# A two-layer graph network: masks laid out by pairs of target tiles, and raw adjacency quarters placed in mask places not yet filled

## The reference

```python
h = jnp.maximum(_layernorm(x, axis=-1), 0.0)
# layer 0
mask = (adj > 0).astype(x.dtype)
agg = mask @ h / jnp.maximum(jnp.sum(mask, axis=1, keepdims=True), 1.0)
combined = jnp.concatenate([h @ W_self + b_self, agg @ W_nb + b_nb], axis=-1)
x = x + jax.nn.relu(combined @ W_comb + b_comb)
h = jnp.maximum(_layernorm(x, axis=-1), 0.0)
# layer 1, per head: Wh = h @ W, sl = Wh . a_l, sr = Wh . a_r
e = jax.nn.leaky_relu(sl[:, :, None] + sr.T[None, :, :], negative_slope=0.2)
e = jnp.where((adj + I > 0)[:, None, :], e, -jnp.inf)
x = x + jax.nn.elu(softmax(e) @ Wh)
```

## Time and profile before

| | |
|---|---|
| median of 3 runs | 873.18 us (868.62 to 874.45) |
| the profiled execution | 872.05 us, span 870.5 us |
| PE busy | 799.2 us, 92% |
| DVE busy | 697.1 us, 80% |
| ACT busy | 564.1 us, 65% |
| transfers | 115.68 MB, mean 133 GB/s |
| first sum of the aggregation, last projection in it | 90.74 us, 369.30 us |

### The profile page before, as it was taken

How to read it: one execution, slowest core, us unless ns; L and a number is a source line. 1 busy time by engine, 2 the same in 40 slices (tenths; PEclk the granted TensorE clock), 3 DMA queues, 4 the chain that set the end, 5 groups by cost and what they waited for, 6 DMA issues and landing times.

```text
span 870.5 us, 26604 instructions
## 1 busy us (share of the span) xinstructions
PE 799.2 (92%) x10789; PEld 726.9 (84%) x10789; DVE 697.1 (80%) x1339; ACT 564.1 (65%) x839; POOL 138.1 (16%) x253
## 2 busy tenths in 40 slices
PE   5896898999999989969999999999999999999995
PEld 4342687778887878759999999999999999999995
DVE  3896766677776676587897999888999889998884
ACT  3574022222222222388999998999989999999991
POOL 0113234444444444400000000000000000000000
PEclk9999799999999999969999999999999999999998
DMA  8645999999999999440041012221101410112001
GB/s 212 181 145 142 281 277 289 285 307 318 316 304 296 300 298 295 101 107 26 1 96 48 2 47 49 49 49 47 48 6 43 96 48 8 41 49 48 9 16 37
DMA packets 91107, 115.68 MB, mean 133 GB/s; under 512 B 62608, under 2 KB 64464, under 8 KB 91056
## 3 DMA queue, kind: packets, MB, share of 16 engines
q1 hardware_dynamic: 70336, 61.57, 26.9%
q10 hardware_dynamic: 10784, 32.65, 13.5%
q0 software_dynamic: 9936, 20.86, 8.4%
HBM read 98.17 MB, written 16.85 MB: 132 GB/s over the span
## 4 chain that ended last, share of the span: by engine, by line
PE 39%; DVE 20%; DMA 17%; ACT 12%; issue 9%; POOL 1%; POOLq 0%; DVEq 0%; ACTq 0%
DMA rows<-own_scratch 14%; ACT stage L752 8%; PE ps_x L623 8%; PE ps_t L623 7%; PE ps_a L623 7%; PE ps_w L623 4%; PE ps_h L623 4%; DVE stage L1046 4%; DVE bits L940 2%; DMA stage<-in_adj 2%; DVE stage L1036 2%; PE ps_a L540 2%; DVE stage L1056 2%; PE ps_t L571 2%; PE ps_t L573 2%
## 5 line engine op out<-in xcount | busy, mean ns | idle before, releaser
L571 PE MATMUL ps_t<-g,mask 128*128 128x257 f16 x1024 | 230.3, 275 | 9.9 <-DVE mask L947 9.9
L573 PE MATMUL ps_t<-g,mask 128*128 128x256 f16 x1024 | 230.2, 273 | 0.0
L752 ACT ACTIVATE stage<-rows,sr 128x1024 int8<-128x1024 f32 x192 | 204.3, 1171 | 5.7 <-PE ps_w L623 5.7
L752 ACT ACTIVATE stage<-bits,sr 128x1024 int8<-128x1024 f32 x192 | 204.3, 1170 | 2.4 <-PE ps_w L623 2.4
L1046 DVE SCALAR_TENSOR_TENSOR stage<-stage,mask 128x1024 int32<-128x1024 int32 x128 | 156.9, 1225 | 22.1 <-ACT stage L752 21.4
L623 PE MATMUL ps_x<-g,stage 128*128 128x130 f16 x2048 | 158.7, 219 | 10.0 <-DVE stage L1056 4.8
L623 PE MATMUL ps_t<-g,stage 128*128 128x130 f16 x2048 | 158.4, 219 | 0.0
L623 PE MATMUL ps_a<-g,stage 128*128 128x130 f16 x2048 | 158.4, 219 | 0.0
L623 PEld LDWEIGHTS ps_x<-g,stage 128*128 128x128 fp8e4 x2048 | 127.4, 97 | 12.1 <-issue 12.0
L623 PEld LDWEIGHTS ps_a<-g,stage 128*128 128x128 fp8e4 x2048 | 127.3, 97 | 0.3
L623 PEld LDWEIGHTS ps_t<-g,stage 128*128 128x128 fp8e4 x2048 | 127.3, 97 | 0.2
(11 more groups left out here) (130 smaller groups left out, 838.9 us busy)
## 6 DMA issues: line engine op xcount, KB each, us to landing
stage<-in_adj SPq DMA_DIRECT2D x134, 256.0 KB, 7.4
stage<-in_adj ACTq DMA_DIRECT2D x122, 256.0 KB, 9.1
own_scratch<-mask POOLq DMA_DIRECT2D x16, 256.0 KB, 2.6
rows<-in_x POOLq DMA_DIRECT2D x128, 32.0 KB, 7.3
rows<-own_scratch POOLq DMA_DIRECT2D x32, 128.0 KB, 9.3
x_scratch<-late POOLq DMA_DIRECT2D x32, 128.0 KB, 7.3
bits<-s_scratch SPq DMA_DIRECT2D x8, 512.0 KB, 4.2
rows<-s_scratch SPq DMA_DIRECT2D x8, 512.0 KB, 4.7
```

The source lines that it names most:

```text
L571: nc.tensor.matmul(ps_t32[e][:, 0:D + 1], at, g[:, 2 * kk + b, D:2 * D + 1], start=kk + b == 0, stop=kk == NK - 1 and b == 1, skip_group_c ...
L573: last = nc.tensor.matmul(ps_t32[e][:, 0:D], at, g[:, 2 * kk + b, 0:D], start=False, stop=kk == NK - 1 and b == 1, skip_group_check=True)
L752: nc.scalar.activation(sign_bytes(sgn, k, b), srow[gr % 2], ACT.Sign, bias=sr[:, 2 * k + b, H + gr // NS:H + gr // NS + 1]).then_inc(act_s ...
```

## The change

The mask is now indexed by pair of target tiles first, then source pair, then the column within the pair: `mask[P, 16, 16, 2P]`. Target pair r has one contiguous row of 8 KB, which is exactly the size of a raw quarter. The prologue's tensors lie in rows 8 to 15 alone. Rows 1 to 7 are free from the start, and raw quarters wait there and, later, in other rows that aren't filled yet. There are 19 places for quarters (16 mask rows and the three of before); `SLOT[n]` names the place of quarter n and `LAST_IN[n]` the quarter that was in it before. `slot_free` holds the waits. SP issues a whole quarter (four parts) with the x rows of each of pairs 4 to 15, quarters 1 to 12, then quarter 13 whole; from 14 on the parts are shared with ScalarE again. ScalarE issues its halves of 14 to 17 at the end of its prologue and the others at the steps that `issued_at` gives.

The x rows of pairs 2 to 15 become one transfer instead of four. On POOL the loops are written out, `own` is fetched ahead of the four parts of x, and a tile's projection is stored ahead of the next tile's x1. The rings in `stage` and `stage2` keep the new order of the mask, with the same number of elements in every operation. `rows` holds own and x of a tile side by side.

Work and bytes are otherwise the same. In the diff blank lines and most context are left out, and the hunk on VectorE's `signs` too, whose only change is the same new view.

```diff
@@ -63,8 +63,8 @@
-ZR = 8
-PR = 4
+ZR = 4
+PR = 2
@@ -96,10 +96,11 @@
-            return mask[:, k, N // 2 + 2 * at:N // 2 + 2 * (at + n)].bitcast(F32)
-        mask = sb("mask", [P, NK, N], U16)
-        mask32 = mask[:, :, :].bitcast(I32)
+            first = NK // 2 * N + k * (N // 2) + 2 * at
+            return mask[:, :, :, :].rearrange("p r k n -> p (r k n)")[:, first:first + 2 * n].bitcast(F32)
+        mask = sb("mask", [P, NK, NK, 2 * P], U16)
+        mask32 = mask[:, :, :, :].bitcast(I32)
@@ -133,10 +134,11 @@
-        halves = [stage[:, 0, :], stage[:, 1, :], stage2[:, :]]
-        rows = sb("rows", [P, 4, D], F32)
-        own = rows[:, 0:2, :]
-        xt = rows[:, 2:4, :]
+        slots = ([mask32[:, r, :, :].rearrange("p k n -> p (k n)") for r in range(NK)]
+                 + [stage[:, 0, :], stage[:, 1, :], stage2[:, :]])
+        rows = sb("rows", [P, 2, 2 * D], F32)
+        own = rows[:, :, 0:D]
+        xt = rows[:, :, D:2 * D]
@@ -169,8 +171,8 @@
-        sgn = stage[:, :, :].rearrange("p f m -> p (f m)").bitcast(I8).rearrange("p (k n) -> p k n", k=ZR)
-        pos = stage2[:, :].rearrange("p (k n) -> p k n", k=PR)
+        sgn = stage[:, :, :].rearrange("p f m -> p (f m)").bitcast(I8).rearrange("p (q r k n) -> p q r k n", q=ZR, r=NJ // 2, k=2)
+        pos = stage2[:, :].rearrange("p (q r k n) -> p q r k n", q=PR, r=NJ // 2, k=2)
@@ -220,7 +222,7 @@
-        stage_in = [sem(f"stage_in{i}") for i in range(3)]
+        raw_in = [sem(f"raw_in{i}") for i in range(NK + 3)]
@@ -296,16 +298,41 @@
-            for a in range(UN):
-                eng.dma_start(xin[k % XR][a * UP:(a + 1) * UP, :], x_v[a, k]).then_inc(x_in[k % XR], 16)
+            if k < 2:
+                for a in range(UN):
+                    eng.dma_start(xin[k % XR][a * UP:(a + 1) * UP, :], x_v[a, k]).then_inc(x_in[k % XR], 16)
+            else:
+                eng.dma_start(xin[k % XR], x_v[:, k]).then_inc(x_in[k % XR], 16)
+        def x_landed(eng, k):
+            eng.wait_ge(x_in[k % XR], k // XR * 16 + (16 * UN if k % XR < 2 else 16))
+        def slot_free(eng, n):
+            if n == EARLY:
+                eng.wait_ge(wmm_ready, 2)
+            elif n == EARLY + 1:
+                eng.wait_ge(ab_ready, 4)
+                eng.wait_ge(consts, 5)
+            elif n == EARLY + 2:
+                eng.wait_ge(h_ready, NK)
+            elif n == EARLY + 3:
+                eng.wait_ge(hT_ready, NK)
+            elif n in (EARLY + 7, EARLY + 8, EARLY + 9):
+                eng.wait_ge(mm_free, 2 * NK + 4)
+            elif n == EARLY + 10:
+                eng.wait_ge(mm_free, 2 * NK + 4)
+                for b in range(2):
+                    eng.wait_ge(own_out[b], 16 * NP2)
+            elif n > EARLY:
+                eng.wait_ge(bits_ready, LAST_IN[n] + 1)
         def adj_rows(eng, n, parts):
-            if n >= 3:
-                eng.wait_ge(bits_ready, n - 2)
+            slot_free(eng, n)
             for a in parts:
-                eng.dma_start(halves[n % 3][a * UP:(a + 1) * UP, :].rearrange("p (e c) -> p e c", e=2),
-                              adj_v[n // UN, n % UN, a]).then_inc(stage_in[n % 3], 16)
+                eng.dma_start(slots[SLOT[n]][a * UP:(a + 1) * UP, :].rearrange("p (e c) -> p e c", e=2),
+                              adj_v[n // UN, n % UN, a]).then_inc(raw_in[SLOT[n]], 16)
@@ -338,10 +365,9 @@
-                if k in (XR, XR + 2):
-                    adj_rows(sp, (k - XR) // 2 + 1, range(UN))
-            for n in range(3, 2 * NT):
-                adj_rows(sp, n, range(UN // 2))
+                adj_rows(sp, k - XR + 1, range(UN))
+            for n in range(NK - XR + 1, 2 * NT):
+                adj_rows(sp, n, range(UN if n < BOTH else UN // 2))
@@ -436,57 +462,42 @@
-            def store_own(k, b):
+            def store_own(k):
                 pool.wait_ge(own_ready, k * 2 + 2)
-                pool.dma_start(own_d[bass.ds(k, 1)].rearrange("o p d -> p (o d)"), ownA[:, b, :]).then_inc(own_out[b], 16)
-            with pool.Fori(0, NP2 - 1) as i:
-                for b in range(2):
-                    store_own(i * 2 + b, b)
-            def row(k, e):
+                pool.dma_start(own_d[k], ownA[:, k % 2, :]).then_inc(own_out[k % 2], 16)
+            def row(t):
+                e = t % 2
+                pool.dma_start(own[:, e, :], own_d[t // 2, :, e * D:(e + 1) * D]).then_inc(row_in[e], 16)
                 for a in range(UN):
-                    pool.dma_start(xt[a * UP:(a + 1) * UP, e, :],
-                                   x_v[a, bass.ds(k, 1), :, e * D:(e + 1) * D].rearrange("o i d -> (o i) d")
+                    pool.dma_start(xt[a * UP:(a + 1) * UP, e, :], x_v[a, t // 2, :, e * D:(e + 1) * D]
                                    ).then_inc(row_in[e], 16)
-                pool.dma_start(own[:, e, :], own_d[bass.ds(k, 1), :, e * D:(e + 1) * D]
-                               .rearrange("o p d -> p (o d)")).then_inc(row_in[e], 16)
-            def store_x1(k, e):
-                pool.wait_ge(x1m_ready, k * 2 + (e + 1))
-                pool.dma_start(x1_d[bass.ds(k * 2 + e, 1)].rearrange("o p d -> p (o d)"), x1[:, e, :]
-                               ).then_inc(x1_out[e], 16)
-            def store_wh(t, e):
+            def store_x1(t):
+                pool.wait_ge(x1m_ready, t + 1)
+                pool.dma_start(x1_d[t], x1[:, t % 2, :]).then_inc(x1_out[t % 2], 16)
+            def store_wh(t):
                 pool.wait_ge(wh_ready, t + 1)
-                pool.dma_start(wh_d[bass.ds(t, 1)].rearrange("o p d -> p (o d)"), wh[:, e, :]
-                               ).then_inc(wh_out[e], 16)
+                pool.dma_start(wh_d[t], wh[:, t % 2, :]).then_inc(wh_out[t % 2], 16)
+            for k in range(NK - 2):
+                store_own(k)
             for b in range(2):
                 pool.wait_ge(own_out[b], 16 * (NP2 - 1))
-            row(0, 0)
-            row(0, 1)
-            for b in range(2):
-                store_own(NK - 2 + b, b)
+            row(0)
+            row(1)
+            store_own(NK - 2)
+            store_own(NK - 1)
             for b in range(2):
                 pool.wait_ge(own_out[b], 16 * NP2)
-            store_x1(0, 0)
-            row(1, 0)
-            with pool.Fori(1, NK - 1) as k:
-                store_x1(k - 1, 1)
-                row(k, 1)
-                store_wh(k * 2 - 2, 0)
-                store_x1(k, 0)
-                row(k + 1, 0)
-                store_wh(k * 2 - 1, 1)
-            store_x1(NK - 2, 1)
-            row(NK - 1, 1)
-            store_wh(NT - 4, 0)
-            store_x1(NK - 1, 0)
-            store_wh(NT - 3, 1)
-            store_x1(NK - 1, 1)
-            store_wh(NT - 2, 0)
+            for t in range(NT):
+                if t:
+                    store_wh(t - 1)
+                store_x1(t)
+                if t + 2 < NT:
+                    row(t + 2)
@@ -567,7 +578,7 @@
-                        at = bytes_of(mask32[:, kk, t // 2 * P:(t // 2 + 1) * P], e, b)
+                        at = bytes_of(mask32[:, t // 2, kk, :], e, b)
@@ -622,7 +633,7 @@
-                            bytes_of(ring[:, k % size, j // 2 * P:(j // 2 + 1) * P], j % 2, b),
+                            bytes_of(ring[:, q % size, j // 2, k % 2, :], j % 2, b),
@@ -704,7 +715,7 @@
-            for n in range(3, 9):
+            for n in range(BOTH, EARLY + 8):
@@ -732,11 +743,11 @@
-                if 2 * t + 9 < 2 * NT:
-                    adj_rows(act, 2 * t + 9, range(UN // 2, UN))
+                for n in issued_at(2 * t):
+                    adj_rows(act, n, range(UN // 2, UN))
-                if 2 * t + 10 < 2 * NT:
-                    adj_rows(act, 2 * t + 10, range(UN // 2, UN))
+                for n in issued_at(2 * t + 1):
+                    adj_rows(act, n, range(UN // 2, UN))
@@ -746,10 +757,10 @@
-                wait_pair(act, gr, q - ZR // 2)
+                wait_pair(act, gr, q - ZR)
-                    nc.scalar.activation(sign_bytes(sgn, k, b), srow[gr % 2], ACT.Sign,
+                    nc.scalar.activation(sign_bytes(sgn, k, b), srow[gr % 2].rearrange("p (r n) -> p r n", n=2 * P), ACT.Sign,
@@ -843,7 +854,7 @@
-                dve.wait_ge(x_in[k % XR], (k // XR + 1) * 16 * UN)
+                x_landed(dve, k)
@@ -934,17 +945,17 @@
-                dve.wait_ge(stage_in[n % 3], (n // 3 + 1) * 16 * UN)
+                dve.wait_ge(raw_in[SLOT[n]], SLOT[:n + 1].count(SLOT[n]) * 16 * UN)
-                                        halves[n % 3].rearrange("p (e m s) -> p e m s", e=2, s=2),
+                                        slots[SLOT[n]].rearrange("p (e m s) -> p e m s", e=2, s=2),
-                nc.vector.transpose(mask32[:, :, n * UP:(n + 1) * UP],
+                nc.vector.transpose(mask32[:, n // UN, :, n % UN * UP:(n % UN + 1) * UP],
@@ -992,7 +1003,7 @@
-                blk = mask32[:, k, k * P:(k + 1) * P]
+                blk = mask32[:, k, k, :]
@@ -1041,20 +1052,21 @@
```

(43 more changed lines are left out.)

## The result

The changed kernel takes 914.99 us in the median of four runs (911.89 to 917.63), beside 872.93 for the kernel before in the same place. The ratio is 1.0489 (95% interval 1.0435 to 1.0543): 4.9% slower, where a gain of 1.6% had been forecast and the range ended at 884. The profiled execution has a span of 915.8 us.

What follows compares the result with a forecast made beforehand. Transfers, full at 299 GB/s, were taken to bound the aggregation, TensorE the attention. First sum 3.8 us later, 18 us of late tiles regained: sums end 14.4 us sooner, 872.05 to 857.7, said as 859 on the median; range 846 to 884.

Steps and rivals of the forecast that it cites:

- The x load: Prologue: x rows of pairs 2 to 15 as one transfer, 0.262 MB a pair; the last ones take 0.9 to 1.2 us.
- the delay of pair 15: End of the prologue: pair 15 starts at 77.8 to 88.9 instead of 72.65, 5 to 16 us late, taken as 10.6.
- The sum: Whole kernel: 872.05 less 14.4 gives 857.7 us, 858.8 on the median, said as 859.
- the last x rows: Prologue: final x rows before pair 15, priced at 0.9 to 1.2 us, with some 1.5 us of landing.
- the other nine portions: Prologue, SP queue: nine per-pair loads of x and a quarter before the last x rows, 5.3 to 6.5 us each.
- Rival B: Prologue: one-piece x runs on four of sixteen engines, 8.5 us a pair, pair 15 36 us late, kernel 881; chance 0.27.
- The queue fill: Prologue: twelve quarters behind x rows make SP's queue the bound, 5.3 to 6.5 us a pair, pair 15 at 77.8 to 88.9.
- The seam: Prologue to first sum: quarter 3 already there, so VectorE's wait goes and 6.8 us come back.
- The sums: Aggregation: 24.2 us of late tiles, of which 6 stay and 18 are regained; sums end at 354.9, 14.4 us sooner.
- Rival C: Aggregation: row loop keeps its beat, tiles stay at 8.73 us, kernel 873; chance 0.12.
- Layout, written-out code, attention: Mask by pairs and unrolled POOL code cost nothing; attention unchanged, moving with the last tile.
- Rival D: Attention: shorter runs make a sign on ScalarE a tenth slower, 18 us net, kernel 877; chance 0.06.

Runs made afterwards that it cites:

- e1: The changed kernel with x rows again in four transfers for every pair: 876.72 us, 1.0035 of the kernel before.
- e3: The changed kernel with the one x transfer taken from 128 consecutive row pairs (other values computed): 879.57 us, 1.0089 of the kernel before.
- e2: The kernel before with only x of pairs 2 to 15 in one transfer of four blocks: 879.93 us, 1.0099.
- e4: The changed kernel with x of pairs 4 to 15 issued by POOL in four transfers, SP issuing quarters only: 876.44 us, 1.0056 of the kernel before.
- e8: e6 with six quarters in the prologue instead of twelve: 853.43 us, 0.9780 of the kernel before.
- e6: e1 with two POOL edits, later wait for the last own stores and rows fetched ahead of the stores: 863.03 us, 0.9896 of the kernel before.
- e5: Changed kernel's mask layout and POOL order alone; x in four transfers, quarters in three places, issued as before: 868.0 us, 0.9962 of the kernel before.
- e9: e5 with the two POOL edits of e6, no early quarters: 870.21 us, 0.9984 of the kernel before.

## Why the prediction was wrong

*The x load.* This step failed: the delay of pair 15, put at 5 to 16 us and taken as 10.6, measured 52.4. The sum took "the last x rows (0.9 to 1.2 us)" for the one-piece load, its bytes at the rate of all engines, and gave its form no price in the other nine portions either. By e1 and e3 the four blocks are worth 38 and 35 us of the kernel; by e2 they take 2.7 us a pair at the rate of about four engines, and on these the quarter and the stores come on top.

Rival B named this mechanism and had too small a price. It took 8.5 us a pair and 36 us of delay. Measured were 8.9 us a pair (33.52 at pair 4 to 113.60 at pair 13) and 52.4. Its own number for x, 3.2 us, lies between the 2.7 of e2 and the 3.5 us of the plateau in the changed kernel. Of the 16 us that it lacks, 4 are the pace (the x rows of pair 15 are issued at 108.38, where B comes to 104.2) and 12 are the way from issue to use, behind what already stood in the queue: 16.6 us, where B allowed 4.7. The lead of four pairs that spoke against B did not help, since the queue was behind at each pair. The rows showed no transfer of this form, so nothing in them bounded its price from above, and a range that ended 3 us beyond B's own number was too narrow.

*The queue fill.* Right in its range once x is out of it: 77.8 to 88.9 was forecast for pair 15, and e1, e3 and e4 have 83.40, 86.6 and 88.0. The point, 83.3 with the first sum at 94.5, was met by e1 to 0.1 us (83.40 and 94.36); that is luck, since it was the middle of a range for which the rows gave no reason. The way there was not as told: the pairs are 4.7 us apart and not about 6, the lead of four pairs being used up meanwhile, and the x rows of pair 15 land late (the last part is issued at 69.39 and used at 83.40). That stores of `own` with two places would become the next wait (e3) was not in the sum. That 12 quarters cannot be had for nothing in the prologue was seen; that six can (e8: 1.8 us) was not worked out, though the earlier trace rows hold it: a pair of 3.47 us at 299 GB/s has room for 1.04 MB, x and own take 0.52, and half a quarter is 0.52. The sum also counts 13 quarters as landed at the first sum; the thirteenth, quarter 12, is issued only behind pair 15.

*The seam.* Forecast 6.8 us, measured 7.1.

*The sums.* Failed too, behind the first. 6 us of late tiles were kept, by e1 it is 22.5: 260.1 us from the first projection to the last one in the sums, less 237.6. "POOL issues the stored rows ahead" was held against late rows, but POOL's wait for two stores (8.0 us over a tile's 7.92 at tile 2 in the changed kernel) and its fetch behind ScalarE's copy weighed nearly as much as the 24.2 before. e6 has 8.2 us over 237.6, near the 6 that were kept, but only with two edits that the change does not have. Rival C had the length of the sums right by luck and not by its mechanism: most tiles of the changed kernel are 7.92 us apart, not 8.73, and a few are much later.

*Layout, written-out code, attention.* Nothing, as costed: e5, and equal rows in attention. Rival D fell.

*The sum.* With x in four transfers (e1) the change ends 0.35% slower than the kernel before (interval -0.08 to +0.78): it loses 10.8 us in front of pair 15, wins 7.1 at the seam, and gains nothing in the sums. So without the four blocks the forecast of 1.6% faster would have missed too, by the sums.

## What to carry to other kernels

Before two prefetches are put on idle transfer engines, work out the room per step in bytes: here half of what was loaded fitted (e8), and the rest delayed the prologue (e1). When a loop over blocks becomes one transfer, look at the outermost dimension of its source: four blocks ran on about four engines and held up everything behind them, a loss of 38 us for 14 transfers. And a deeper prefetch shows its gain only where the next wait in line, here the rows and two stores on the third queue, is loosened with it: e6's edits gave nothing alone (e9), twelve early quarters gave nothing alone (e1), both together gave 1.0% (e6), and with six quarters instead of twelve 2.2% (e8). Six quarters without the edits were not run.

## What the runs showed of the hardware

- A transfer with four blocks of 64 KB at the source moved 98 to 111 GB/s for most of e2's stretch, with the sixteen engines busy at 2 tenths; the same bytes as 128 row pairs, or in four transfers, left no such plateau.
- SP's issue of a transfer, 0.59 us as a rule, took up to 6.3 us in the changed kernel, where its queue was behind.
- A store of 256 KB by POOL landed in 2.6 us (median) in the kernel before. In the full prologue of e3 it took 8.3 to 8.8 us, and 14 to 16 us in the changed kernel when both other queues had just been given 27 parts of quarters between them.
- From 45 to 65 us the transfers ran at 290 and 291 GB/s whether x was on POOL's or SP's queue (e4, e1). In e8, at 286 GB/s and the same full share, pair 15 began only 1.8 us later than before.
